# Loads at the heads of two attention stages: the first two units' loads are issued in front, ScalarE issues some of them, and group 0's keys come strip by strip

## The chip, the cores and the metric

One core of one Trainium2 chip runs the whole program. The metric is the device time of one execution in microseconds (us). The core has the engines PE (TensorE), DVE (VectorE), ACT (ScalarE), POOL (GpSimd) and SP (SyncE), and 16 DMA engines that all of them share. SP does nothing but issue DMAs; POOL and ACT can issue them too. Every engine runs its own instructions strictly in order, and a wait on a semaphore holds everything that is behind it on that engine.

## The reference

Two transformer layers over 4096 tokens of 256 features, 16 heads of 16. Layer 0 is a strided and local attention (each query sees every 8th key of the whole sequence and the keys of its own block of 128) beside an fp8 product; layer 1 is two dense causal attentions beside a mixture of experts. Cut to what the change touches:

```python
# layer 0, sparse: strided keys and the query's own block, one softmax over both
k_str = k[:, :, :Lg].reshape(B, Hn, ns, GBL, d)[:, :, :, -1, :]
w = softmax(einsum('bhnqd,bhnkd->bhnqk', fq, concat(k_str, k_local)) * scale + mask)
o = einsum('bhnqk,bhnkd->bhnqd', w, concat(v_str, v_local))
# layer 1, dense, twice (rotary q and k; normalised q and k)
scores = einsum('bhqd,bhkd->bhqk', Q, K) / sqrt(16);  causal mask;  softmax;  @ V
```

## The kernel before

The program has five stages that follow each other: embedding and the first projection, the sparse attention (`attend((0,), "sparse", ...)`), the middle projections, the two dense attentions (`attend((1, 2), "dense", ...)`), and the experts. At the end of each stage all five engines wait for all of its work and its stores (`stage_end`), so a stage's loads can't be issued before the stage ahead of it has stored its last bytes.

`attend` works on **units**: 4 heads (a group) of one strip of 512 queries. The sparse stage has 32 units (4 groups of 8 strips), the dense one 64. What a unit needs:

- its queries, in 6 DMAs of 64 KB (three terms for the odd and the even heads), into one of `held` buffers; in the sparse stage also its own keys (6 DMAs) and own values (1), which is 13 DMAs a unit;
- the keys and values of its group: strided keys and values in the sparse stage (`load_strided`, 7 DMAs a group, all four groups resident), the group's 4096 keys and values in the dense stage (two buffers; group 0's first strip of keys by 6 DMAs on SP, the other seven strips and the values by POOL, and group 1 by POOL as soon as unit 0 is weighed);
- rows of ones under the keys (`load_ones`, 2 rows for the odd and the even heads of each key tile) and mask halves (`load_halves`).

Each unit goes through two passes. First PE makes the unit's scores in **tiles** (L772 and L779 sparse, L783 dense), and DVE takes the maximum of each (L909, L913, L916). DVE negates the maxima, PE turns them (L788), DVE copies them to `neg_rows` (L937), and SP carries them by two small DMAs into two more rows of the unit's queries: this is the unit's **hand** (L713). Only then can PE make the scores again with the maximum already subtracted (L822, L832 sparse, L813 dense), ACT takes the exponential (L873) and PE multiplies by the values (L853). The list `order`, which all engines follow, lets the tiles run ahead of the second pass by `lead(n)` chunks. At the start of the sparse stage that is the 20 tiles of unit 0 and 8 of unit 1, at the start of the dense stage the 16 tiles of unit 0 and 24 of unit 1. In `order` a unit's first tile stands behind an entry `queries` for the next unit, at which SP issues that unit's loads; the hand of unit n stands at the sixth tile of unit n + 1.

## Time and profile before

| | |
|---|---|
| median of 3 runs | 5220.52 us (5220.5 to 5229.52) |
| the profiled execution | 5214.47 us, of which the span of the profile is 5212.6 us |
| busy share of the span | PE 91%, DVE 78%, ACT 54%, POOL 5% |
| sparse stage | from about 216 us to 840 us |
| dense stage | from about 1219 us to 4460 us |

The times in the profile count from the start of the span. "SPq" is SP's instruction queue issuing DMAs, and the granted clock (PEclk) is a share of 2.4 GHz, so 0.50 is 1.2 GHz and 1.00 is 2.4 GHz. A DMA's landing is the time when all of its bytes are counted in its semaphore.

### The profile page before, as it was taken

The numbers are of one execution on the slowest core, as the hardware profiler recorded it, in microseconds if no ns is written. First come the engines' busy times: TensorE is split into PE (matmuls) and PEld (weight loads), VectorE is DVE, ScalarE is ACT, GpSimd is POOL, SyncE is SP. The second block draws the span as 40 slices with busy tenths as digits, with TensorE's granted clock in tenths as the row PEclk, the third lists the DMA queues.
The fourth block names the chain that finished last, engine by engine and source line by source line (L and its number), as shares of the span: only waits on it lengthen the run. The fifth ranks groups of instructions, "written<-read, shape, count | busy, mean of one in ns | idle before, by whom it ended". The sixth has DMA issues, their size and how long they took to land.

```text
span 5212.6 us, 82823 instructions
## 1 busy us (share of the span) xinstructions
PE 4765.6 (91%) x31872; PEld 2545.8 (49%) x31872; DVE 4064.0 (78%) x9211; ACT 2835.7 (54%) x3309; POOL 270.1 (5%) x329
## 2 busy tenths in 40 slices
PE   5599997774999999999999999999999999899999
PEld 4455555662443334433334443334433333688888
DVE  7677775774888998889998889998889976455555
ACT  3255553221456766566766666766666776322322
POOL 2100001332000000000000000000000000200000
PEclk8699998776789999999999999999999999899999
DMA  5532322555300030300201300201300000210010
GB/s 162 171 79 66 70 69 83 187 175 145 58 13 13 7 55 23 54 9 9 46 12 23 54 9 9 46 12 23 54 9 9 5 9 11 70 41 21 21 41 9
DMA packets 256956, 258.37 MB, mean 50 GB/s; under 512 B 77224, under 2 KB 197032, under 8 KB 255016
## 3 DMA queue, kind: packets, MB, share of 16 engines
q1 hardware_dynamic: 250032, 211.50, 14.4%
q0 software_dynamic: 6528, 41.55, 5.0%
q8 instruction: 252, 4.13, 0.3%
q14 instruction: 144, 1.18, 0.1%
HBM read 145.43 MB, written 105.97 MB: 48 GB/s over the span
## 4 chain that ended last, share of the span: by engine, by line
PE 70%; DVE 18%; issue 5%; ACT 1%; DMA 1%; SPq 1%; POOL 0%; DVEq 0%; ACTq 0%; POOLq 0%
PE psum L853 23%; PE psum L783 19%; PE psum L76 13%; DVE maxes_dense L916 11%; PE psum L813 4%; PE psum L745 3%; PE psum L772 2%; PE psum L793 1%; PE psum L822 1%; PE psum L1596 1%; DVE masked_scores_dense L909 1%; PE psum L779 1%; PE psum L1197 1%; DMA queries_dense<-parts_scratch 1%; PE psum L1576 0%
## 5 line engine op out<-in xcount | busy, mean ns | idle before, releaser
L873 ACT ACTIVATE probs_dense<-psum 128x1024 f32<-128x1024 f32 (+3 forms) x2304 | 2068.2, 950 | 985.2 <-PE psum L813 741.8
L916 DVE TENSOR_REDUCE maxes_dense<-psum 128x1 f32<-128x512 f32 x3584 | 2226.7, 683 | 217.1 <-PE psum L783 216.2
L783 PE MATMUL psum<-keys,queries_dense 48*128 48x512 f32 (+3 forms) x4608 | 1551.1, 475 | 140.4 <-DMA queries_dense<-parts_scratch 56.2
L783 PEld LDWEIGHTS psum<-keys,queries_dense 48*128 48x128 f32 x4608 | 664.9, 190 | 1489.7 <-DVE maxes_dense L916 1137.8
L853 PE MATMUL psum<-probs_dense,values 128*32 128x512 f32 (+3 forms) x9216 | 1171.2, 586 | 0.0
L813 PE MATMUL psum<-queries_dense,keys 50*128 50x512 f32 (+3 forms) x4608 | 804.6, 405 | 12.2 <-ACT probs_dense L873 11.9
L909 DVE CUSTOM_DVE_ANT_0 masked_scores_dense<-psum,causal_add 128x128 f32<-128x128 f32 (+3 forms) x1024 | 452.4, 488 | 178.2 <-PE psum L783 159.2
L813 PEld LDWEIGHTS psum<-queries_dense,keys 50*128 50x128 f32 x4608 | 446.6, 192 | 107.3 <-ACT probs_dense L873 61.5
L909 DVE CUSTOM_DVE_ANT_0 masked_scores_sparse<-psum,after_add 128x512 f32<-128x512 f32 x512 | 326.1, 687 | 94.5 <-PE psum L772 93.5
L1703 ACT ACTIVATE activated<-psum 128x512 f32<-128x512 f32 x208 | 124.6, 599 | 417.6 <-PE psum L76 407.8
L853 PEld LDWEIGHTS psum<-probs_dense,values 128*32 128x32 f32 x9216 | 189.5, 109 | 270.9 <-issue 205.9
L873 ACT ACTIVATE probs_sparse<-psum 128x1024 f32<-128x1024 f32 x224 | 217.2, 1022 | 129.1 <-PE psum L745 51.8
L772 PE MATMUL psum<-str_keys,queries_sparse 48*128 48x512 f32 x512 | 176.2, 502 | 51.7 <-DMA str_values<-v_scratch 23.2
L1838 DVE CAST hid_high<-activated 128x512 fp32r<-128x512 f32 x208 | 92.2, 443 | 143.9 <-ACT activated L1703 140.9
L1840 DVE TENSOR_TENSOR hid_low<-activated,hid_high 128x512 fp32r<-128x512 f32 x208 | 150.4, 723 | 7.2
L772 PEld LDWEIGHTS psum<-str_keys,queries_sparse 48*128 48x128 f32 x512 | 70.7, 191 | 167.9 <-DVE maxes_sparse L909 88.2
L745 PE MATMUL psum<-tri_key,eye_bf 64*128 64x128 bf16 x2048 | 147.4, 223 | 0.0
L853 PE MATMUL psum<-probs_sparse,str_values 128*32 128x512 f32 x1024 | 142.4, 629 | 0.0
L873 ACT ACTIVATE probs_sparse<-psum,after_bias 128x1024 f32<-128x1024 f32 x96 | 101.6, 1112 | 66.1 <-PE psum L822 66.1
L822 PE MATMUL psum<-queries_sparse,str_keys 50*128 50x512 f32 x512 | 123.5, 450 | 1.5 <-ACT probs_sparse L873 1.3
L645 POOL DMA_DIRECT2D keys<-parts_scratch x48 | 24.1, 508 | 1931.5 <-PE psum L853 1917.7
L913 DVE TENSOR_REDUCE maxes_sparse<-psum 128x4 f32<-128x512 f32 x128 | 83.1, 688 | 44.5 <-PE psum L779 43.7
(295 smaller groups left out, 5350.6 us busy)
## 6 DMA issues: line engine op xcount, KB each, us to landing
v_scratch<-ve_s SPq DMA_DIRECT2D x96, 256.0 KB, 2.7
parts_scratch<-part_high SPq DMA_DIRECT2D x24, 1024.0 KB, 4.2
parts_scratch<-part_low SPq DMA_DIRECT2D x24, 1024.0 KB, 6.8
queries_dense<-parts_scratch SPq DMA_DIRECT2D x384, 64.0 KB
keys<-parts_scratch POOLq DMA_DIRECT2D x42, 512.0 KB, 18.0
values<-v_scratch POOLq DMA_DIRECT2D x8, 2048.0 KB, 34.9
queries_sparse<-parts_scratch SPq DMA_DIRECT2D x192, 64.0 KB
own_keys<-parts_scratch SPq DMA_DIRECT2D x192, 64.0 KB
```

Source lines behind the costliest of these rows:

```text
L76: m = pe.matmul(out_ap, left(l, c), right(r, c), start=(n == 0), stop=(n == len(pairs) - 1))
L745: m = pe.matmul(bank, eye2[own, part, :], addend, start=start and part == 0, stop=stop and part == 1)
L772: m = pe.matmul(bank, q[rows(h, TROWS), h // 2, b * P:(b + 1) * P], str_keys[n // STRIPS][rows(h, TROWS), h // 2, :], start=True, stop=True)
L783: m = pe.matmul(bank[:, 0:width], q[rows(h, TROWS), h // 2, b * P:(b + 1) * P], k[rows(h, TROWS), h // 2, kc * STRIP:kc * STRIP + width], ...
L813: m = pe.matmul(full[:, first_col:STRIP], k[own, h // 2, c * P:(c + 1) * P], q[own, h // 2, first_col:STRIP], start=True, stop=not diagonal)
L822: m = pe.matmul(full, str_keys[n // STRIPS][own, h // 2, c * P:(c + 1) * P], q[own, h // 2, :], start=True, stop=not partly)
L853: m = pe.matmul(psum[own_rows, 4, cols], vt, probs[(2 * m_at + h // 2) % 6][:, h % 2, cols], start=(c == 0), stop=(c == sizes[n] - 1 and b ...
L873: act.activation(probs[i % 6][:, :, first_col:STRIP], psum[:, at2:at2 + 2, first_col:STRIP], ACT.Exp, scale=SCALE, **extra).then_inc(exp_d ...
L909: m = dve.tensor_tensor_reduce(out=masked_scores[e % 2][:, 0:width], in0=bank[:, 0:width], in1=mask, scale=1.0, scalar=-3e38, op0=ALU.add, ...
L916: m = dve.tensor_reduce(mx[:, h * BLOCKS + b, kc:kc + 1], bank, AX.X, ALU.max)
L1703: act.activation(gs[k % 2][:], h_bank(u), func).then_inc(activated, 1)
L1840: dve.tensor_tensor(low[:, f, :], g[:], high[:, f, :].bitcast(F32), ALU.subtract).then_inc(hid_split, 1)
```

## The change

Five edits, all at the heads of the two attention stages:

1. SP issues the loads of unit 0 and unit 1 first in both stages, and from then on the entry `queries` for unit n + 1 issues the loads of unit n + 2. The sparse stage holds 6 units' tiles instead of 4 (the dense one held 8 already).
2. In the sparse stage ACT issues group 0's strided keys and values and all rows of ones (now 20 DMAs of ones, for 6 own key tiles); SP keeps the strided loads of groups 1 to 3.
3. In the dense stage group 0's keys come with the queries: each of the units 0 to 7 brings the strip of keys with its own number, by 6 more DMAs on SP. POOL's load of strips 1 to 7 is gone, and POOL issues group 0's values only when unit 1's loads have landed.
4. In the dense stage the masks and the ones are issued behind unit 1's loads, and PE waits for them at unit 0's second pass, no longer ahead of the first tile.
5. ACT issues the four weight loads ahead of the dense stage that SP issued before.

```diff
-        held = 4 if sparse else 8
+        held = 6 if sparse else 8
...
+                    if not sparse and n < STRIPS:
+                        load_keys(sp, 0, slice(j * STRIP, (j + 1) * STRIP), queries_in[n % 8])
...
+                load_queries(0)
+                load_queries(1)
                 if sparse:
-                    load_queries(0)
-                    load_strided(0)
-                    for tile in with_ones:
-                        load_ones(tile, ones_in)
                     for g in range(1, GROUPS):
-                        load_strided(g)
+                        load_strided(sp, g)
                 else:
                     for tile, name in halves:
                         load_halves(tile, name, masks_in)
                     for tile in with_ones:
-                        load_ones(tile, masks_in)
-                    load_keys(sp, 0, slice(0, STRIP), first_keys_in)
-                    load_queries(0)
+                        load_ones(sp, tile, masks_in)
                 for kind, n, what in order:
-                    if kind == "queries" and n < len(units):
-                        load_queries(n)
+                    if kind == "queries" and n + 1 < len(units):
+                        load_queries(n + 1)
...
-                else:
-                    pe.wait_ge(masks_in, 16 * mask_loads)
...
+                        if not sparse and n == 0:
+                            pe.wait_ge(masks_in, 16 * mask_loads)
...
             def attend_act():
                 if sparse:
+                    load_strided(act, 0)
+                    for tile in with_ones:
+                        load_ones(act, tile, ones_in)
                     act.wait_ge(bias_set, 1)
...
                 if not sparse:
-                    load_keys(pool, 0, slice(STRIP, TOKENS), keys_in[0])
+                    pool.wait_ge(queries_in[1], count_loaded(1))
                     load_values(pool, 0)
                     load(1)
...
-        sp.dma_start(tile, src).then_inc(final_weights, 16)
+        act.dma_start(tile, src).then_inc(final_weights, 16)
```

On SP at the head of the sparse stage, before: a unit's loads end with `own_values`, a group's strided loads with `str_values`. The stretch begins at the last own keys of unit 0.

```order
L679 DMA own_keys_0<-parts_scratch0_0 16x2x512
L681 DMA own_values_0<-v_scratch0 128x4x128
L658 DMA str_keys_0<-strided_scratch0 16x2x512
L658 DMA str_keys_0<-strided_scratch1 16x2x512
...
L660 DMA str_values_0<-v_scratch0 128x4x128
L637 DMA str_keys_0<-ones_scratch 2x2x512 x2
...
L637 DMA own_keys_3<-ones_scratch 2x2x512 x2
L658 DMA str_keys_1<-strided_scratch0 16x2x512
...
L660 DMA str_values_3<-v_scratch0 128x4x128
L672 DMA queries_sparse_1<-parts_scratch0_0 16x2x512 x2
```

The same place on SP now, with the way down to the hand of unit 0 (L721; L713 before).

```order
L691 DMA own_keys_0<-parts_scratch0_0 16x2x512
L693 DMA own_values_0<-v_scratch0 128x4x128
L682 DMA queries_sparse_1<-parts_scratch0_0 16x2x512 x2
...
L693 DMA own_values_1<-v_scratch0 128x4x128
L668 DMA str_keys_1<-strided_scratch0 16x2x512
...
L670 DMA str_values_3<-v_scratch0 128x4x128
L682 DMA queries_sparse_2<-parts_scratch0_0 16x2x512 x2
...
L682 DMA queries_sparse_3<-parts_scratch0_0 16x2x512 x2
...
L693 DMA own_values_3<-v_scratch0 128x4x128
L721 DMA queries_sparse_0<-neg_rows_sparse_0 2x8x128 x2
```

Unit 1's loads stand directly behind unit 0's, the strided loads of group 0 and the ones have left the queue, and four units' loads (before: three) stand ahead of the first hand.

On SP at the head of the dense stage, before, from the four weights of L1469 to the hand of unit 0.

```order
L1469 DMA lower<-in_c_lower 128x16
L146 DMA eye2_bf<-in_c_ident_bf 64x2x128 x2
L146 DMA tri_key2<-in_c_tri_key 64x2x128 x2
L637 DMA keys_0<-ones_scratch 2x8192 x2
L637 DMA keys_1<-ones_scratch 2x8192 x2
L645 DMA keys_0<-parts_scratch1_0 16x2x512
...
L672 DMA queries_dense_0<-parts_scratch1_0 16x2x512 x2
...
L672 DMA queries_dense_2<-parts_scratch1_1 16x2x512
L713 DMA queries_dense_0<-neg_rows_dense_0 2x8x128 x2
```

The same place on SP now; between the queries of each unit and the next stand six DMAs of keys (L655).

```order
L682 DMA queries_dense_0<-parts_scratch1_0 16x2x512 x2
...
L655 DMA keys_0<-parts_scratch1_0 16x2x512
L682 DMA queries_dense_1<-parts_scratch1_0 16x2x512 x2
...
L146 DMA eye2_bf<-in_c_ident_bf 64x2x128 x2
L146 DMA tri_key2<-in_c_tri_key 64x2x128 x2
L647 DMA keys_0<-ones_scratch 2x8192 x2
L647 DMA keys_1<-ones_scratch 2x8192 x2
L682 DMA queries_dense_2<-parts_scratch1_0 16x2x512 x2
...
L682 DMA queries_dense_3<-parts_scratch1_0 16x2x512 x2
...
L721 DMA queries_dense_0<-neg_rows_dense_0 2x8x128 x2
```

Ahead of the first tile's data SP had 18 other DMAs (4 weights, 4 masks, 4 ones and the 6 of the first key strip, which the tile needs) and now has none but the 12 that it needs; ahead of the first hand stand 48 loads of units and the 8 of masks and ones, before 4 + 8 + 6 + 18.

On POOL at the head of the dense stage, before and then now (the wait is in the diff).

```order
L645 DMA keys_0<-parts_scratch1_0 16x2x3584
L645 DMA keys_0<-parts_scratch1_1 16x2x3584
L645 DMA keys_0<-parts_scratch1_0 16x2x3584 x2
L645 DMA keys_0<-parts_scratch1_1 16x2x3584
L645 DMA keys_0<-parts_scratch1_0 16x2x3584
L650 DMA values_0<-v_scratch1 128x32x128
L645 DMA keys_1<-parts_scratch1_0 16x2x4096
```

```order
L660 DMA values_0<-v_scratch1 128x32x128
L655 DMA keys_1<-parts_scratch1_0 16x2x4096
```

The six large loads of group 0's keys are gone from POOL; group 1's follow as they did.

## Rows read from the trace of the kernel before

**Rows 1.** The page's part 4: the chain that ended last, by engine.

```profile
PE 70%; DVE 18%; issue 5%; ACT 1%; DMA 1%; SPq 1%; POOL 0%; DVEq 0%; ACTq 0%; POOLq 0%
```

**Rows 2.** The chain in order of time at the sparse head: start us, us, what.

```profile
224.65 3.05 DMA str_values<-v_scratch
...
227.84 0.81 PE psum L772 x2
...
242.54 11.71 issue
254.26 0.81 PE psum L772 x2
...
258.81 0.20 DVE neg_rows_sparse L937
...
259.72 1.94 DMA queries_sparse<-neg_rows_sparse
```

**Rows 3.** Timeline of SP's queue at the sparse head: start us, us, what, count.

```profile
215.79 2.66 SPq L672 DMA_DIRECT2D queries_sparse<-parts_scratch  x6
...
225.12 5.17 SPq L637 DMA_DIRECT2D str_keys<-ones_scratch  x8
...
235.34 2.73 SPq L658 DMA_DIRECT2D str_keys<-strided_scratch  x6
...
245.41 2.84 SPq L672 DMA_DIRECT2D queries_sparse<-parts_scratch  x6
...
251.55 2.83 SPq L672 DMA_DIRECT2D queries_sparse<-parts_scratch  x6
...
259.03 1.31 SPq L713 DMA_DIRECT2D queries_sparse<-neg_rows_sparse  x2
```

**Rows 4.** The chain in order of time at the dense head: start us, us, what.

```profile
1230.25 3.89 SPq L672
...
1237.25 28.80 DMA queries_dense<-parts_scratch
...
1266.28 0.49 PE psum L783 x2
...
1288.36 0.46 PE psum L813 x2
...
1293.98 1.86 PE psum L853 x8
```

**Rows 5.** Timeline of SP's queue at the dense head.

```profile
1219.45 0.37 SPq L1469 DMA_DIRECT2D wo<-in_L_ffn_wo  x1
...
1221.36 1.73 SPq L146 DMA_DIRECT2D eye_bf<-in_c_ident_bf  x2
...
1226.16 2.65 SPq L645 DMA_DIRECT2D keys<-parts_scratch  x6
1228.85 29.49 SPq L672 DMA_DIRECT2D queries_dense<-parts_scratch  x18
1278.63 1.41 SPq L713 DMA_DIRECT2D queries_dense<-neg_rows_dense  x2
```

**Rows 6.** Timeline of POOL at the dense head.

```profile
1223.20 1.72 POOL L650 DMA_DIRECT2D values<-v_scratch  x1
1302.00 2.98 POOL L645 DMA_DIRECT2D keys<-parts_scratch  x6 [77.08 <-PE psum L853]
```

**Rows 7.** Stretches: from:to and length, busy us by engine, PEclk, DMA share, GB/s.

```profile
1240.00:1245.00 5.00, 0.00 (x0) 0.00 (x0) 0.00 (x0) 0.00 (x0) 0.00 (x0) 0.50 1.00 117
...
1250.00:1252.00 2.00, 0.00 (x0) 0.00 (x0) 0.00 (x0) 0.00 (x0) 0.00 (x0) 0.50 1.03 375
...
1262.00:1264.00 2.00, 0.00 (x0) 0.00 (x0) 0.00 (x0) 0.00 (x0) 0.00 (x0) 0.50 0.08 27
```

**Rows 8.** Stretches, as above: a stretch of the sparse head, and one behind the dense head.

```profile
245.00:250.00 5.00, 0.00 (x0) 0.00 (x0) 0.00 (x0) 0.00 (x0) 0.00 (x0) 0.50 0.70 175
...
1300.00:1700.00 400.00, 389.15 (x2248) 164.73 (x2245) 352.29 (x718) 219.96 (x247) 16.70 (x23) 0.86 0.15 27
```

More of the change, by code:

```diff
@@ L518, in attend, with count_loaded, handed @@
         sparse = jobs == (0,)
-        held = 4 if sparse else 8
-        loads = 16 * (13 if sparse else 6)
-        per_unit = loads + 32
-        earlier = 0 if sparse else 4 * (16 * 13 + 32)
+        held = 6 if sparse else 8
+        per_unit = 16 * 15 if sparse else 16 * 8
+        earlier = 0 if sparse else 4 * 16 * 15
+        def count_loaded(n):
+            if sparse:
+                return per_unit * (n // 8) + 16 * 13
+            return earlier + per_unit * (n // 8) + 16 * 12
+        def handed(n):
+            return count_loaded(n) + 32
         groups = [(a, g) for a in jobs for g in range(GROUPS)]
@@ L598, in attend @@
                 keys_in, values_in = ([sem(f"{k}_in{i}") for i in range(2)] for k in ("keys", "values"))
-                first_keys_in, masks_in = sem("first_keys_in"), sem("masks_in")
+                masks_in = sem("masks_in")
             side_filled, side_freed = sem(f"side_filled_{stage}"), sem(f"side_freed_{stage}")
@@ L632, in attend, with load_ones @@
                 with_ones = keys
-            def load_ones(tile, loaded):
+            def load_ones(queue, tile, loaded):
                 for odd in range(2):
                     first_row = odd * HALF + TROWS
-                    sp.dma_start(tile[first_row:first_row + MROWS, :, :].bitcast(F32), ones_d[:, :, 0:tile.shape[2]]).then_inc(loaded, 16)
+                    queue.dma_start(tile[first_row:first_row + MROWS, :, :].bitcast(F32), ones_d[:, :, 0:tile.shape[2]]).then_inc(loaded, 16)
             def load_keys(queue, group, tokens, loaded):
@@ L650, in load_values, with load_strided @@
                 queue.dma_start(values[group % 2][:], v_d[a][g].rearrange("(b p) n -> p b n", p=P)).then_inc(values_in[group % 2], 16)
-            def load_strided(g):
+            def load_strided(queue, g):
                 for odd in range(2):
@@ L657, in load_strided @@
                         first_row = odd * HALF + i * HEAD_DIM
-                        sp.dma_start(str_keys[g][first_row:first_row + HEAD_DIM, :, :].bitcast(F32),
+                        queue.dma_start(str_keys[g][first_row:first_row + HEAD_DIM, :, :].bitcast(F32),
                                      src.rearrange("(h o e) t -> o e h t", o=2, e=HEAD_DIM)[odd]).then_inc(str_in[g], 16)
-                sp.dma_start(str_values[g][:], v_d[0][g].rearrange("(c p e) n -> p c e n", p=P, e=STRIDE)
+                queue.dma_start(str_values[g][:], v_d[0][g].rearrange("(c p e) n -> p c e n", p=P, e=STRIDE)
                              [:, :, STRIDE - 1, :]).then_inc(str_in[g], 16)
@@ L723, in wait_keys @@
                 group = n // STRIPS
-                if group == 0:
-                    pe.wait_ge(first_keys_in, 96)
-                    if n >= 1:
-                        pe.wait_ge(keys_in[0], 96)
-                else:
-                    pe.wait_ge(keys_in[group % 2], 96 * (group // 2 + 1))
+                if group >= 1:
+                    pe.wait_ge(keys_in[group % 2], 96 * ((group + 1) // 2))
             def attend_pe():
@@ L749, in attend_pe @@
                     pe.wait_ge(sparse_masks_in, SPARSE_MASKS)
-                else:
-                    pe.wait_ge(masks_in, 16 * mask_loads)
                 for kind, n, what in order:
@@ L765, in attend_pe @@
                         if what == tiles_of(n)[0]:
-                            pe.wait_ge(queries_in[n % 8], earlier + per_unit * (n // 8) + loads)
+                            pe.wait_ge(queries_in[n % 8], count_loaded(n))
                             if sparse:
@@ L935, in attend_dve @@
                         if n >= 2:
-                            dve.wait_ge(queries_in[(n - 2) % 8], earlier + per_unit * ((n - 2) // 8 + 1))
+                            dve.wait_ge(queries_in[(n - 2) % 8], handed(n - 2))
                         dve.tensor_copy(neg_rows[n % 2][:], psum[0:MROWS * GROUP * BLOCKS, 5 + e % 3, 0:P]).then_inc(side_freed, 1)
```

2 lines of the change are left out of this document (1 added, 1 removed).

## Prediction

> **What bounds the kernel now.** The page's chain first: 70% of the span goes over PE and 18% over DVE [rows 1]. So the long stretches of the five stages are bound by matmuls and maxima, which the change leaves alone: not one is added or taken away. What it can reach is the part of the chain that goes over DMAs and idle issue, and the chain in order of time shows that part in two places, the heads of the two attention stages.
>
> At the sparse head the chain runs over a landing at 224.65 + 3.05 = 227.70 us, then PE starts on the tiles of unit 0 at 227.84, is done with them at 242.54, and stands for 11.71 us until unit 1's loads have landed [rows 2]. SP's queue shows why these are late: unit 1's loads are issued from 245.41 on, behind the ones (from 225.12) and three groups' strided loads (from 235.34) [rows 3]. The second pass starts only when unit 0's hand has landed, at 259.72 + 1.94 = 261.66 [rows 2].
>
> At the dense head SP starts to issue at 1219.45 [rows 5] and PE at 1266.28, released by a load of queries that ends a wait of 28.80 us for the DMA alone [rows 4]. Here it is not SP that is slow at first: a single issue of L672 took 3.89 us [rows 4], and 18 of them 29.49 us [rows 5], where six issues took 2.66 us in the sparse stage [rows 3]. All 16 DMA engines were busy (share 1.00) while they moved only 117 GB/s [rows 7]; that is POOL's load of seven strips of keys, which was issued ahead of the queries and crowds them out. From 1288.36 on unit 0's second pass runs, and from 1293.98 on its values are used [rows 4].
>
> Both heads are behind a barrier of all engines, so a microsecond won at a head moves everything behind it, as long as no other wait takes its place. Each sum below therefore asks when the **second pass of unit 0** can start, since by then PE has done the same 28 (sparse) or 40 (dense) tiles in either kernel.
>
> **Sparse head.** SP's order is now unit 0, unit 1, three strided groups, unit 2, unit 3, hand of unit 0. A unit's 13 issues take 251.55 - 245.41 = 6.14 us, the three strided groups 245.41 - 235.34 = 10.07 us [rows 3]. Unit 0's loads have been issued at 215.79 + 6.14 = 221.9 and land some 3 us after their last issue (3.05 us is the row's value for such a landing [rows 2]), at about 224.7. Unit 1's are issued by 228.1 and land by 231. PE starts some 3 us sooner than at 227.84, needs 14.7 us for unit 0's tiles (242.54 - 227.84 [rows 2]), reaches 239.5, and finds unit 1 there: the stall of 11.71 us is gone. The turned maxima were ready 258.81 + 0.20 - 254.26 = 4.8 us after unit 1's first tile [rows 2], so now at about 244.3. But a new wait takes a share of it: SP is free for the hand only at 215.79 + 4 x 6.14 + 10.07 = 250.4. Before it issued the hand at 259.03 [rows 3], at once. The gain is 259.0 - 250.4 = 8.6 us, not the 15 that the data alone would give. As the hand now stands right behind 26 loads in the same queue, I take 8. The bounds: 14.7 if nothing stood ahead of the hand (259.0 - 244.3), and below, the case of the rivals in which ACT's issues slow SP's.
>
> What ACT now issues has cover. No row shows an issue on ACT. If it costs what SP's do (0.44 us for a strided one, 5.17 / 8 = 0.65 us for one of ones [rows 3]), its 7 strided DMAs are out at 219 and its 20 of ones at 232; at three times that the strided loads are out at 225 and the ones at 264, and only the ones would then be later than the hand. Its first exponential comes behind the hand.
>
> The DMA engines had a share of 0.70 at 175 GB/s while SP issued without a pause [rows 8], so issue time, not bandwidth, set the pace, and ACT's 7 large DMAs can overlap for some 3 us. The Trainium skill ("DMA: Bandwidth & Descriptors", section "Issuing engines are not separate DMA queues") says that DMAs from different engines run on the same 16 DMA engines and that issuing from several saves only the sequencer's time, which it calls usually small. By the rule taken alone this edit would win nothing; by the row the saved time is what counts, since the queue of issues is 34.6 us long. Both agree that only issue time can be saved, and the sum holds nothing else.
>
> **Dense head.** Twelve issues are needed for unit 0. Six take 1228.85 - 1226.16 = 2.69 us where nothing crowds them [rows 5], so twelve 5.4. They start at 1219.45, end at 1224.8, and land 3 us after their last issue, at 1227.5; I give ACT's four weights beside them half a microsecond. PE starts at 1228.0 in place of 1266.28: **38.3 us** sooner. Unit 1's loads are out at 1230.2 and land at 1233, while PE needs 8 us for unit 0's tiles.
>
> Then the hand. Behind unit 1 SP issues masks and ones in 1226.16 - 1221.36 = 4.8 us [rows 5], then unit 2 and unit 3 (5.4 each), and is free at 1245.8. Before, the hand was issued 1278.63 - 1266.28 = 12.4 us after the first tile [rows 4, 5], which would be 1240.4: again it waits in SP's queue. It lands 2.6 us after its issue (261.66 - 259.03 [rows 2, 3]), at 1248.4. PE comes to the second pass 1288.36 - 1266.28 = 22.1 us after the first tile [rows 4], at 1250.1. So on paper the delay is hidden with 1.7 us to spare.
>
> Two things can eat that. First POOL's values: 2 MB at the 375 GB/s of [rows 7] are 5.6 us, and they start at about 1235, as units 2 and 3 are issued. Second the ones: in the dense stage each is 64 KB in only two rows. After POOL's traffic the DMA share was 0.08, little more than one of 16 engines, while the last loads of SP were still outstanding [rows 7]; these landed at 1237.25 + 28.80 = 1266.05 [rows 4]. My reading is that the four DMAs of ones hold one or two engines for long, an estimate of 6 to 10 us, and that what SP issued behind them waits there. Now they stand behind units 0 and 1, which is a gain, but ahead of the hand: 1235 + 10 = 1245, then what is left of the loads of units 2 and 3 and of the values, and the hand lands at 1251 to 1255. I take 3 us of loss against 1250.1, with 0 and 9 as bounds. Values: needed 1293.98 - 1266.28 = 27.7 us after the first tile [rows 4], at 1255.7 or later; issued at 1233 to 1235 (1.72 us [rows 6]), they may land from 1242 to 1254. Before, they also carried no wait. Dense gain: 38.3 - 3 = **35 us**.
>
> **Costed at nothing.** The 6 further DMAs for units 2 to 7 cost SP 2.7 us each in a queue that otherwise waits for hands; their cover is the length of a unit. From unit 4 on they fall into POOL's load of group 1, which starts with the end of unit 0 (before at 1302.00 [rows 6]) as it did; unit 2's hand would be the first to suffer. Loading two units ahead needs a free buffer: by the order of the program each buffer is released by a product that PE has already passed, so SP waits for nothing new. Four weights on ACT lie 60 us ahead of its first exponential. PE's later wait for the masks is met at 1240.
>
> **Sum.** 8 + 35 = 43 us. The profiled execution took 5214.47 us, so it would be 5171.5; the median of the runs is 5220.52, 6 us more, and the forecast is 5220.5 - 43 = **5177.5 us**, 0.8% faster. Within 0.2% (some 10 us) a measurement of this kernel can't tell from no change.
>
> **The rivals.**
>
> *The dense hand is crowded out.* If the issues of unit 3 are held as SP's were before (3.89 us each [rows 4] in place of 0.45), twelve cost 41 us more and the dense gain is gone: 5220.5 - 8 = 5212. Against it: POOL's keys are not there, and 2 MB of values last a fifth of that. A part is likelier: 10 us lost give 5187. Together 14%.
>
> *ACT and SP get in each other's way as they issue.* If the hardware behind both took one issue at a time, ACT's 7 and 20 (3.1 + 13 us) would push the sparse hand to 266, 7 us later than before: 5220.5 + 7 - 35 = 5192. Nothing in this trace shows ACT issuing, for or against. 8%.
>
> *The first tile's data land no sooner,* since the stage's bytes must come in anyway. Then only the sparse 8 us are left, 5212. Against it: at the sparse head the same kind of loads landed in 3 us. 3%.
>
> *Slower: PE's clock.* It was granted 0.50 over both heads, and 0.86 on average from 1300 to 1700 [rows 8], with PE busy for 389 of 400 us. In the new kernel PE comes to this stretch with a shorter rest behind it. If the clock were granted less there, PE's time would grow in proportion: 400 x 0.86 / x - 400 exceeds 43 us when x falls under 0.777, and at 0.70 it would be 91 us, 5269 in all. Against it: the stretch holds the same matmuls in the same order. 3%.
>
> **How the numbers follow.** The forecast (36 to 52 us won, 5168 to 5185) has 70%, more than that 2%. The range 5165 to 5193 takes in the forecast, the partly crowded hand and the shared issue. Faster by over 0.2%: 0.93; within: 0.04; slower: 0.03.
>
> **What the profile after would show.** Right: PE's first L772 near 225 us and no long gap before unit 1's tiles; the sparse hand issued near 250 with SP never idle before it; dense first tile 8 to 9 us after SP's first issue of the stage; no issue of SP over 1 us before POOL's values; PE waiting a few microseconds for the dense hand; a clock from there on as before. Wrong: issues of 2 us and more on SP for units 2 and 3, a wait of PE for values, or issues on SP beside ACT's that are longer than 0.5 us. I am surest of the 38 us and least sure of the hand behind the ones.

## Result and the profile after

| | before | the changed kernel |
|---|---|---|
| median of 14 runs each | 5230.78 us (5207.63 to 5257.79) | 5198.48 us (5184.92 to 5222.99) |
| profiled execution, its span | 5214.47, 5212.6 us | 5203.78, 5201.9 us |
| ratio, 95% interval | | 0.9941 [0.9922, 0.9959] |

The change makes the kernel about 31 us faster (1 - 0.9941 of 5230.78; 41 to 21 by the interval), where 43 were forecast. In a later comparison (12 and 23 runs) the ratio was 0.9958 [0.9939, 0.9978], 22 us.

**Sparse head.** Timeline of SP's queue in the changed kernel, then of ACT's, then the two rows of PE at which the first tile and the second pass of unit 0 become possible (the bracket is the idle time before and its releaser):

```profile
215.78 2.67 SPq L682 DMA_DIRECT2D queries_sparse<-parts_scratch  x6
218.49 3.23 SPq L691 DMA_DIRECT2D own_keys<-parts_scratch  x6
221.76 0.59 SPq L693 DMA_DIRECT2D own_values<-v_scratch  x1
222.39 3.72 SPq L682 DMA_DIRECT2D queries_sparse<-parts_scratch  x6
...
230.55 3.27 SPq L668 DMA_DIRECT2D str_keys<-strided_scratch  x6
...
242.19 2.83 SPq L682 DMA_DIRECT2D queries_sparse<-parts_scratch  x6
...
254.49 1.51 SPq L721 DMA_DIRECT2D queries_sparse<-neg_rows_sparse  x2
```

```profile
215.81 2.74 ACTq L668 DMA_DIRECT2D str_keys<-strided_scratch  x6
218.59 0.45 ACTq L670 DMA_DIRECT2D str_values<-v_scratch  x1
219.07 5.60 ACTq L647 DMA_DIRECT2D str_keys<-ones_scratch  x8
224.70 7.85 ACTq L647 DMA_DIRECT2D own_keys<-ones_scratch  x12
```

```profile
229.91 1.19 PE L774 MATMUL psum<-str_keys,queries_sparse 48*128 48x512 f32 x3 [25.24 <-DMA own_values<-v_scratch]
...
257.43 0.80 PE L774 MATMUL psum<-str_keys,queries_sparse 48*128 48x512 f32 x2 [7.65 <-DMA queries_sparse<-neg_rows_sparse]
```

The stall for unit 1's loads is gone, and PE waits 7.65 us for the hand. But the first tile comes 2.1 us later than before (229.91 against 227.84 [rows 2]), and six issues on SP take 3.72 us beside ACT's, in place of 2.66. The wait for the hand ends at 257.4, before at 261.7 [rows 2]: 4.3 us won. Windows of before and then of the changed kernel (length, busy by engine, PEclk, DMA share, GB/s) show why the data come no sooner:

```profile
220.00:225.00 5.00, 0.00 (x0) 0.00 (x0) 0.00 (x0) 0.00 (x0) 0.00 (x0) 0.50 0.76 177
```

```profile
220.00:225.00 5.00, 0.00 (x0) 0.00 (x0) 0.00 (x0) 0.00 (x0) 0.00 (x0) 0.50 1.14 161
225.00:230.00 5.00, 0.09 (x2) 0.12 (x2) 0.00 (x0) 0.00 (x0) 0.00 (x0) 0.50 1.13 175
```

Two queues issue, the DMA engines are busier (a share of 1.14 in place of 0.76), and they move no more bytes in a second than one queue fed them before (161 and 175 GB/s in place of 177).

**Dense head.** SP's queue, POOL and PE in the changed kernel, then the one link of its chain that matters:

```profile
1218.48 2.66 SPq L682 DMA_DIRECT2D queries_dense<-parts_scratch  x6
...
1232.28 1.34 SPq L647 DMA_DIRECT2D keys<-ones_scratch  x4
1233.66 4.24 SPq L682 DMA_DIRECT2D queries_dense<-parts_scratch  x6
...
1246.70 1.41 SPq L721 DMA_DIRECT2D queries_dense<-neg_rows_dense  x2
```

```profile
1231.95 1.86 POOL L660 DMA_DIRECT2D values<-v_scratch  x1 [26.58 <-DMA keys<-parts_scratch]
```

```profile
1227.48 0.76 PE L785 MATMUL psum<-keys,queries_dense 48*128 48x128 f32 x3 [18.32 <-DMA keys<-parts_scratch]
...
1260.30 0.48 PE L785 MATMUL psum<-keys,queries_dense 48*128 48x128 f32 x2 [11.54 <-DMA queries_dense<-neg_rows_dense]
1260.57 0.74 PE L817 MATMUL psum<-queries_dense,keys 50*128 50x512 f32 x2
```

```profile
1247.44 12.81 DMA queries_dense<-neg_rows_dense
```

The same second-pass row of before, in PE's timeline, was

```profile
1287.89 1.00 PE L813 MATMUL psum<-queries_dense,keys 50*128 50x512 f32 x2
```

The first tile comes 9.0 us after SP's first issue of the stage (46.8 before), the hand is issued 19.2 us after the tile, and then these two DMAs of 8 KB take 12.81 us to land (counted here and below from the start of the second one's issue, where the chain has it). The second pass starts 42.1 us after SP's first issue (1260.57 - 1218.48), before 68.4 (1287.89 - 1219.45 [rows 5]): 26.3 us won. Both heads together: 4.3 + 26.3 = 30.6 us, which agrees with the runs (21 to 41 us).

**What the dense hand waits for.** The trace also keeps the time of each increment of each semaphore, and these show it. The loads in 16 rows and the values raise their semaphore 16 times for each DMA. The DMAs of two rows, the ones and the hand, raise it 3 times, once at the issue and twice later. In the changed kernel the last increment of the ones comes at 1247.43, just as the hand's second DMA is issued, so the hand doesn't wait for the ones themselves. But of the 16 increments of the values 14 have come by 1248.16 and the last two come at 1256.27 and 1256.53. The last of unit 2's loads comes at 1257.33, of unit 3's at 1259.89 and of the hand at 1260.25. Two parts of sixteen are 8 us behind, and the hand lands with them. In e9, the changed kernel once more, it is the same (14 by 1259.49, then 1266.89 and 1268.62), and in e12 below, where the ones have another shape, all 16 come between 1255.65 and 1258.04. The values' DMA as a whole shows it too: from its issue to its landing it takes 24.8 us in e9 and 15.4 in e12.

**Where the rest of the time went.** The two profiled executions differ by only 10.7 us, so 19.9 us of the 30.6 were lost outside the heads: 3.3 ahead of the dense head and 16.6 behind it. One stretch behind it, in before and then in the changed kernel:

```profile
3055.00:3230.00 175.00, 170.83 (x1142) 70.06 (x1144) 157.28 (x305) 119.98 (x133) 0.00 (x0) 0.98 0.03 7
```

```profile
3055.00:3230.00 175.00, 171.25 (x1063) 69.48 (x1063) 150.22 (x292) 114.56 (x126) 0.00 (x0) 0.91 0.05 10
```

PE is as busy in both, but at 0.91 of full speed in place of 0.98 it does 1063 matmuls in place of 1142. In the profiled execution of e9 14.8 us were lost much earlier, between the hands of units 5 and 7 of the sparse stage. The times of all runs follow their mean granted clock: of the changed kernel's 14 runs the fastest (5184.92 us) had 0.932 and the slowest (5222.99 us) 0.924. So the spread of 38 to 50 us in the times of either kernel goes with the clock, and the experiments are read by distances within the heads, where the clock is 0.50; a single time says little.

### The profile page after: what moved, and what is told of

Read it like the earlier page. It is cut to its first block, busy times and chain, and to the rows that moved or that the text cites. A ratio compares the mean times of both kernels' runs of the same rounds, so it can differ in the third digit from the quotient of the medians.

```text
span 5201.9 us, 82855 instructions
## 1 busy us (share of the span) xinstructions
PE 4783.6 (92%) x31872; PEld 2548.6 (49%) x31872; DVE 4063.9 (78%) x9211; ACT 2836.0 (55%) x3309; POOL 268.0 (5%) x323
## 3 DMA queue, kind: packets, MB, share of 16 engines
q1 hardware_dynamic: 250304, 212.87, 14.5%
## 4 chain that ended last, share of the span: by engine, by line
PE 71%; DVE 18%; issue 4%; ACT 1%; SPq 1%; DMA 1%; POOL 0%; DVEq 0%; ACTq 0%; POOLq 0%
PE psum L857 23%; PE psum L785 19%; PE psum L76 13%; DVE maxes_dense L923 11%; PE psum L817 4%; PE psum L749 3%; PE psum L774 2%; PE psum L795 1%; PE psum L826 1%; PE psum L1603 1%; DVE masked_scores_dense L916 1%; PE psum L781 1%; PE psum L1204 1%; PE psum L1583 0%; PE psum L836 0%
## 5 line engine op out<-in xcount | busy, mean ns | idle before, releaser
L817 PE MATMUL psum<-queries_dense,keys 50*128 50x512 f32 (+3 forms) x4608 | 807.1, 406 | 11.8 <-ACT probs_dense L880 11.5
L826 PE MATMUL psum<-queries_sparse,str_keys 50*128 50x512 f32 x512 | 122.8, 450 | 1.5 <-ACT probs_sparse L880 1.3
L920 DVE TENSOR_REDUCE maxes_sparse<-psum 128x4 f32<-128x512 f32 x128 | 83.2, 688 | 45.1 <-PE psum L781 44.3
L655 POOL DMA_DIRECT2D keys<-parts_scratch x42 | 20.8, 503 | 1891.6 <-PE psum L857 1891.4
```

The costliest lines, as they stand in the source:

```text
L817: m = pe.matmul(full[:, first_col:STRIP], k[own, h // 2, c * P:(c + 1) * P], q[own, h // 2, first_col:STRIP], start=True, stop=not diagonal)
L826: m = pe.matmul(full, str_keys[n // STRIPS][own, h // 2, c * P:(c + 1) * P], q[own, h // 2, :], start=True, stop=not partly)
```

## The experiments

All kernels are the changed one but for the edit shown, and each was run once, but for e8 and e9. Where PE didn't wait for the hand (before, e1, e6, e8), its landing is the last increment of its semaphore. Dense head, us; "from SP" is from SP's first issue of the stage, the others from PE's first tile:

| kernel | first tile from SP | hand issued | hand landed | second pass | second pass from SP |
|---|---|---|---|---|---|
| before | 46.8 | 12.4 | 15.0 | 21.6 | 68.4 |
| changed | 9.0 | 19.2 | 32.8 | 33.1 | 42.1 |
| changed, again (e9) | 9.7 | 18.3 | 32.9 | 33.2 | 42.9 |
| e1 ones behind the hand | 9.2 | 18.0 | 21.6 | 32.0 | 41.2 |
| e2 values behind the hand | 9.6 | 17.1 | 22.5 | 22.8 | 32.4 |
| e3 unit 3 behind the hand | 9.3 | 12.8 | 30.1 | 30.4 | 39.7 |
| e5 ones by strip | 8.9 | 23.1 | 25.7 | 26.0 | 34.9 |
| e6 values at once | 15.1 | 12.4 | 18.7 | 21.6 | 36.7 |
| e10 half the ones | 9.5 | 17.3 | 25.9 | 26.2 | 35.8 |
| e12 ones spread | 9.8 | 21.2 | 24.7 | 25.0 | 34.9 |
| e8 five moves together | 10.1 | 14.1 | 16.6 | 22.9 | 33.0 |

The edits of e4, e7 and e11 leave the dense head as it is, and there its second pass comes 42.6, 41.2 and 43.1 us after SP's first issue, so a distance of this head varies by 2 us.

Sparse head, us from SP's first issue of the stage:

| kernel | first tile | hand issued | second pass (L822, now L826) |
|---|---|---|---|
| before | 12.1 | 43.2 | 46.5 |
| changed (e9) | 14.1 (14.4) | 38.7 (40.1) | 42.2 (43.5) |
| e3 unit 3 behind the hand | 14.2 | 33.5 | 38.9 |
| e4 ones from 18 us on | 12.8 | 37.7 | 45.1 |
| e7 16 of 20 ones behind the hand | 14.0 | 35.5 | 41.8 |
| e11 ACT issues nothing | 12.5 | 50.7 | 54.1 |
| e8 five moves together | 14.1 | 33.4 | 36.8 |

In the six dense experiments that leave this head as it is, its second pass comes 41.9 to 44.0 us after SP's first issue. So the change wins 2.5 to 4.6 us here, and a difference of 2 us between two kernels says nothing.

**e1: the ones of the dense keys behind the first hand**

```diff
-                    for tile in with_ones:
-                        load_ones(sp, tile, masks_in)
...
+                        if not sparse and n == 0:
+                            for tile in with_ones:
+                                load_ones(sp, tile, masks_in)
```

> Dense head only: the four DMAs of ones are issued behind the hand of unit 0, not ahead of the loads of units 2 and 3. In the changed kernel the hand was issued at 1246.70 and landed at 1260.25, 32.8 us after PE's first tile, where 22.1 us would have kept PE busy. Theory A (the ones hold the two DMA engines that the hand also needs): the hand is issued some 1.3 us sooner and lands within 5 us of its issue, by about 23 us after the first tile; PE then waits for the ones, not for the hand, some 10 us more, so the second pass starts about where it did. Theory B (the loads of units 2 and 3 and the values crowd the hand): the hand still lands 10 us or more after its issue. Theory C (issue time on SP): it lands 1.3 us sooner, no more.

5204.75 us. The hand lands 21.6 us after the tile, 2.9 us after its last issue, with the values and the loads of units 2 and 3 where they were; so these alone don't make it late. But the second pass needs the ones too, and they are slow behind it. PE and the chain:

```profile
1272.68 0.47 PE L786 MATMUL psum<-keys,queries_dense 48*128 48x128 f32 x2 [10.53 <-DMA keys<-ones_scratch]
```

```profile
1261.56 11.03 DMA keys<-ones_scratch
```

Four DMAs of 64 KB take 11 us from their last issue, while the last of the keys, as large each and in 16 rows, landed in 3.98 us in the same run. By the increments the four land one after the other, at 1265.56, 1268.09, 1270.53 and 1272.60.

**e2: POOL issues the values behind the first hand**

```diff
-                    pool.wait_ge(queries_in[1], count_loaded(1))
+                    pool.wait_ge(queries_in[0], handed(0))
```

> Dense head only: POOL issues group 0's values (2 MB) when the hand of unit 0 has landed. Theory A (ones): the hand still lands 10 us or more after its issue, at most 3 us sooner than the 32.8 us after the first tile. Theory B, for its part on values: it lands within 5 us, some 8 to 10 us sooner. In either case the products of unit 0 wait for values, by about 8 us after the hand's landing, so the time as a whole is not better than the changed kernel's.

5169.15 us. The ones stand where they stood, and the hand lands after 4.64 us, 22.5 after the tile; then the values are late. The chain:

```profile
1248.40 4.64 DMA queries_dense<-neg_rows_dense
...
1253.68 10.12 DMA values<-v_scratch
```

So the ones alone are done by the time of the hand (their last increment is at 1247.02). It takes the values as well to make it late.

**e3: unit 3's loads behind the first hand, in both stages**

```diff
-                    if kind == "queries" and n + 1 < len(units):
+                    if kind == "queries" and n != 2 and n + 1 < len(units):
...
+                        if n == 0:
+                            load_queries(3)
```

> Both heads: the loads of unit 3 are issued behind the hand of unit 0, not ahead of it. Sparse: the hand goes out when its rows are ready, about 249, not at 254.49, and the second pass starts about 5 us sooner, at 252. Dense: the hand is issued near 1241 (relative to a stage start at 1218.48; 12 us after the first tile). Theory A (ones): it lands when the ones are through, 27 to 31 us after the first tile, against 32.8, since fewer loads stand between. Theory B (loads and values crowd it) the same or better, 23 to 27. Theory C (SP's issue time alone was what made it late): 15 to 18 us after the first tile, and PE doesn't wait for it at all.

5210.46 us. In the dense stage the hand is issued 6.4 us sooner after the tile and lands 2.7 us sooner (16.54 us under way): it isn't SP's queue that decides there. In the sparse stage the same move wins 3.3 us at the second pass (38.9 against 42.2, and 3.0 against the lowest of the unchanged heads).

**e5: each unit's strip of dense keys brings its own ones**

```diff
+                        for odd in range(2):
+                            first_row = odd * HALF + TROWS
+                            sp.dma_start(keys[0][first_row:first_row + MROWS, :, j * STRIP:(j + 1) * STRIP].bitcast(F32),
+                                         ones_d[:, :, 0:STRIP]).then_inc(queries_in[n % 8], 16)
...
-                    for tile in with_ones:
-                        load_ones(sp, tile, masks_in)
...
+                        if not sparse and n == 0:
+                            sp.wait_ge(masks_in, 64)
+                            load_ones(sp, keys[1], masks_in)
```

> Dense head: the rows of ones of group 0's key tile come strip by strip, two DMAs of 8 KB with each unit's keys, and those of the other key tile (128 KB) only behind the hand of unit 0. So two rows' worth of 32 KB less each, four times, stands on the two DMA engines ahead of the hand; the values stay as they were. Earlier runs gave for the hand's landing, counted from PE's first tile: 32.8 us in the changed kernel, 30.1 with the hand issued 6 us sooner, 22.5 with the values issued behind it. Theory F (ones and values add up on two engines, either one's removal frees the hand): the hand lands 22 to 25 us after the first tile, and PE waits 3 us at most. Theory B alone (the values' packets slow everything by themselves): 28 us or later. The second pass of unit 0 would start 8 to 10 us sooner than the changed kernel's 33.3 us after the first tile under F, 3 us or less under B.

5184.48 us. With the values where they were and only 8 KB of ones in a DMA (two DMAs a unit), the hand is issued 23.1 us after the tile and lands at once:

```profile
1255.20 1.87 DMA queries_dense<-neg_rows_dense
```

**e6: POOL issues the values without a wait**

```diff
-                    pool.wait_ge(queries_in[1], count_loaded(1))
```

> Dense head: POOL issues group 0's values at once, without the wait for unit 1's loads. Under theory F the 2 MB pass while units 0 and 1 are loaded: the first tile comes later than the 9.0 us after SP's first issue that the changed kernel has, by up to 8 us, and the hand then finds the engines free but for the ones: it lands within 6 us of its issue. Sum: second pass of unit 0 at 36 to 40 us after SP's first issue of the stage, against 42.3 in the changed kernel. If the values crowd out the first loads as group 0's keys did in the kernel before (SP's issues of 3 us and more), it is 45 or later.

5211.4 us. The first tile pays 6 us (15.1), and the second pass is yet 5.4 us sooner from SP's first issue (36.7 against 42.1): the values' last increment comes at 1243.99, while the ones are being issued (1242.70 to 1244.03), and PE doesn't wait for the hand at all.

**e10: half the ones.** keys_1's two DMAs behind the first hand, keys_0's two in place.

> Of the dense stage's four large DMAs of ones only keys_0's two stand ahead of unit 2's loads; keys_1's two go behind the first hand. Theory A (the large two-row DMAs hold the engines on which they run, and their time adds to the values' ahead of the hand): half the ones, about half of their 11 us gone, so the hand of unit 0 lands 26 to 29 us after the first tile (changed kernel 32.8) and PE waits 5 to 8 us in place of 11.5. Rival (the values and the loads of units 2 and 3 alone make the hand late): it lands 31 to 33 us after the first tile as before. A second rival (any two-row load ahead is enough, whatever its size): the same 31 to 33.

5181.15 us. The hand lands 25.9 us after the tile, 6.9 us sooner; PE waits 4.70 us.

**e12: the same ones, in the same place, in another shape.** 8 DMAs of one row in 16 pieces (1x16x512) in place of 4 of two rows (2x8192):

```diff
+                        for odd in range(2):
+                            for r in range(MROWS):
+                                row = odd * HALF + TROWS + r
+                                sp.dma_start(tile[row:row + 1, :, :].bitcast(F32).rearrange("s h (b c) -> s (h b) c", c=512),
+                                             ones_d.rearrange("s g t -> (s g t)").rearrange("(o c e) -> o c e", o=1, e=1024)[:, :, 0:512]).then_inc(masks_in, 16)
```

> The same 256 KB of ones for the dense keys, at the same place in SP's queue, but as 8 DMAs of one row in 16 pieces (1x16x512) in place of 4 of two rows (2x8192). Computes the same. Theory A (the bytes of a two-row DMA run on very few DMA engines, and the hand, two rows too, waits there): in 16 pieces the ones are spread and cost nothing; SP issues four more DMAs (about 1.5 us), so the hand is issued 20 to 21 us after the first tile and lands 2 to 5 us behind, 22 to 26 us after the tile, PE waits 0.5 to 4 us (changed kernel 32.8 and 11.5). Rival (the bytes ahead of the hand and the values crowd it, whatever their shape): it lands 32 to 34 us after the first tile, as in the changed kernel.

5179.95 us. SP's queue, PE and the chain:

```profile
1241.92 5.55 SPq L714 DMA_DIRECT2D keys<-ones_scratch  x8
...
1259.23 1.41 SPq L725 DMA_DIRECT2D queries_dense<-neg_rows_dense  x2
```

```profile
1262.73 0.47 PE L789 MATMUL psum<-keys,queries_dense 48*128 48x128 f32 x2 [3.47 <-DMA queries_dense<-neg_rows_dense]
```

```profile
1259.98 2.70 DMA queries_dense<-neg_rows_dense
```

The same 256 KB in the same place of the queue, with the values beside them, and the hand lands 2.70 us after its last issue in place of 12.81. The issues cost more (0.69 us each in place of 0.34), and PE waits 3.47 us. The shape was the cause, not the number of bytes. (The new DMAs also read their source in pieces of 2 KB with gaps; this wasn't tried apart from the spread.)

**e4: ACT's ones only when unit 1's loads have landed (sparse)**

```diff
                     load_strided(act, 0)
+                    act.wait_ge(queries_in[1], count_loaded(1))
```

> Sparse head only: ACT issues group 0's strided loads at once, but its 20 DMAs of ones only when unit 1's loads have landed. In the changed kernel SP's issues of unit 1 took 8.16 us beside ACT's ones, against 6.14 before, and own_values landed only at 229.8. Theory D (issues from two engines slow each other): SP's issues for unit 1 take 6.2 us again, unit 0's tiles start 2 to 4 us sooner than 229.91, and the hand is issued 3 to 4 us sooner than 254.49 if ACT's ones don't then slow the strided groups instead; if they do, 0 to 1 us. Theory E (the DMA engines are the limit, not the issuing): SP's issues stay at 0.57 us each.

5224.68 us. SP's timeline in this run, ahead of ACT's ones and then while ACT issues them (234.43 to 247.90):

```profile
222.23 2.83 SPq L682 DMA_DIRECT2D queries_sparse<-parts_scratch  x6
...
239.02 3.72 SPq L682 DMA_DIRECT2D queries_sparse<-parts_scratch  x6
```

The longer issues move with ACT's ones. The hand is issued 1.0 us sooner but takes 6.00 us to land (2.04 in the changed kernel), so the head as a whole loses 2.9. Here too two parts of sixteen lag: of a weight load that SP issued right behind the hand 14 increments have come by 257.72 and the last two come at 260.75 and 261.75. The first tile comes 1.3 us sooner than in the changed kernel, so ACT's ones are the larger part of the 2.1 us that it lost.

**e7: ACT issues 4 of the ones, the other 16 behind the first hand (sparse)**

```diff
+                    for tile in (str_keys[0], keys[0]):
+                        load_ones(act, tile, ones_in)
+                    act.wait_ge(queries_in[0], handed(0))
...
+                    for tile in str_keys[1:] + keys[1:]:
+                        load_ones(act, tile, ones_in)
```

> Sparse head: ACT issues the strided loads of group 0 and only the 4 DMAs of ones that unit 0 needs; the other 16 when unit 0's hand has landed. Theory D (issues of small two-row DMAs on ACT make SP's issues longer, 0.57 to 0.60 us in place of 0.43 to 0.47): nearly all of SP's issues go back to 0.43 to 0.47 us, the hand is issued 34.5 to 35.5 us after SP's first issue of the stage, against 38.7, and lands within 3 us; the second pass starts 3 to 4 us sooner than in the changed kernel. The first tile stays where it is, 13 to 14 us after SP's first issue (12.05 in the kernel before), if the DMA engines limit the landing of unit 0's 20 loads. Theory E (issuing isn't what is slowed): the hand's issue stays within 1 us of 38.7.

5229.54 us. SP is back at 0.43 to 0.47 us an issue and issues the hand 3.2 us sooner, but it takes 4.79 us to land, and the second pass gains 0.4, which is nothing clear. No two parts lag clearly here (the 16 increments of the same weight load come from 255.09 to 257.42); the DMA engines had a share of 1.08 at 203 GB/s (250 to 255 us), and the hand lands at 257.24, just after unit 3's loads at 256.86. Then ACT's first exponential stands behind its 16 issues, and unit 0's outputs are ready 14.5 us later than in the changed kernel (74.8 against 60.3 us after SP's first issue).

**e11: ACT issues nothing at the sparse head; SP does all**

```diff
                 load_queries(0)
+                if sparse:
+                    load_strided(sp, 0)
                 load_queries(1)
+                if sparse:
+                    for tile in with_ones:
+                        load_ones(sp, tile, ones_in)
```

> At the sparse head ACT issues nothing; SP issues unit 0, group 0's strided loads, unit 1, the 20 ones and from there on as the changed kernel. Theory D (issue time counts, and SP's issues lengthen only beside ACT's): SP's issues fall back to 0.45 us, but 27 more stand in its queue; 4 units at 6.14, 4 strided groups at 3.3 and 20 ones at 0.65 us are 51 us, so the hand is issued 50 to 52 us after SP's first issue (changed kernel 38.7), lands 3 us behind, and the second pass starts at about 269.5 us, 12 us later than in the changed kernel and 8 later than before the change. Rival (the bytes ahead of the hand set its landing, whoever issues them): the second pass starts at 257 to 259 us.

5216.9 us. The hand is issued 50.7 us after SP's start, and the second pass starts at 270.82. Issue time in front of the hand does count: ACT's 27 issues would take SP 16.1 us (3.34 + 12.72 in this run) and moving them to ACT brings the hand 12.0 sooner.

**e8: five moves together, beside the changed kernel (e9), 12 runs each.** Ones by strip as in e5; unit 3's loads behind the hand as in e3; the strided groups 1 to 3 one each behind the hands of units 0 to 2; the values as soon as unit 0's loads have landed, not unit 1's:

```diff
-                    pool.wait_ge(queries_in[1], count_loaded(1))
+                    pool.wait_ge(queries_in[0], count_loaded(0))
...
+                        if sparse and n + 1 < GROUPS:
+                            load_strided(sp, n + 1)
```

> Computes the same as the changed kernel. Five moves beside it: in the dense stage each unit's strip of keys brings its own 8 KB of ones (4 rows in two DMAs), the other key tile's large ones go behind the first hand; unit 3's loads go behind the first hand in both stages; the strided groups 1 to 3 of the sparse stage are loaded one each behind the hands of units 0 to 2; POOL issues the values once unit 0's loads have landed, not unit 1's. Theory A (the large two-row ones, and what is queued in the DMA engines ahead of the hand, set its landing): the dense second pass starts 31 to 33 us after SP's first issue of the stage (changed kernel 42.3), the sparse hand is issued about 34 us after SP's first issue (changed kernel 38.7) and the second pass of unit 0 comes about 5 us sooner than in the changed kernel. Together 10 to 15 us under the changed kernel, a ratio to before of 0.991 to 0.992. Rival (the hand's place decides nothing, each head is bound by the stage's bytes): second passes at the same distances as in the changed kernel, and the same time as it within 0.1%.

> The changed kernel again, on the same chip as the kernel above, so that the two can be compared: 0.992 to 0.996 of before, as in its first runs, with the dense second pass 42 us and the sparse one 41 to 42 us after SP's first issue of the stage.

e8: 5203.4 us, ratio to before 0.9928 [0.9902, 0.9955]; e9: 5214.96 us, 0.9958 [0.9939, 0.9978]. The heads of e8 win 35.4 + 9.7 = 45.1 us over before, those of e9 25.5 + 3.0 = 28.5; both lie in their intervals. By the heads e8 is 16.6 us faster than the changed kernel, by the medians 11.6, but the intervals overlap, so the times alone don't tell them apart. Time multiplied by the run's granted clock does, as it takes out most of the spread: on average 4823.4 for e9 and 4815.1 for e8, 8.4 apart with a standard error of 2.3, where 16.6 us at a clock of 0.50 would be 8.3. At the dense head PE no longer waits for the hand; unit 1's ones hold it for 1.96 us, and DVE's maxima set the rest of the way:

```profile
1236.10 0.77 PE L791 MATMUL psum<-keys,queries_dense 48*128 48x128 f32 x3 [19.46 <-DMA keys<-ones_scratch]
...
1245.02 1.19 PE L791 MATMUL psum<-keys,queries_dense 48*128 48x512 f32 x3 [1.96 <-DMA keys<-ones_scratch]
...
1258.98 1.00 PE L825 MATMUL psum<-queries_dense,keys 50*128 50x512 f32 x2
```

## Why the prediction was too high

**Dense first tile, 38.3 us: right.** 8 to 9 us after SP's first issue were forecast and 9.0 came, so the tile is 37.8 us sooner (46.8 - 9.0). That POOL's load of seven strips was what had crowded the queries out is argued and not shown alone: in the kernel before, of the 96 increments of unit 0's queries 84 came by 1259.29 and the last 12, two of sixteen for each DMA, only from 1264.81 to 1266.04. So some 7 us of its 46.8 are the two lagging parts behind the ones, and the change took away both at once. ACT's four weights cost nothing visible.

**The dense hand, "3 us of loss, with 0 and 9 as bounds": the step that failed.** The mechanism was named, the ones ahead of the hand and then the values, but its size was not. The loss was 33.1 - 21.6 = 11.5 us, above my upper bound. I had the hand wait until 1245 for the ones and let what is left of units 2 and 3 and of the values follow until 1251 to 1255. The ones did end near there (1247.43), but what follows took until 1260.25. Behind the ones the values and the units' loads had piled up on the engines that carry them, by the increments two of sixteen, and I had priced that rest without this. So the two add up: ones without values ahead leave the hand at 22.5 (e2), values without ones at 21.6 (e1, hand issued at 18.0), both together at 32.8, half the ones at 25.9. And e12 shows that it is the shape: cut in 16 pieces, the same ones cost the hand nothing beyond their issue time. A row that the prediction had in hand, a share of 0.08 while the last loads were outstanding [rows 7], pointed there. I read it as one or two engines busy, and then did not ask on which engines the hand itself, also two rows, would run.

The Trainium skill ("DMA: Bandwidth & Descriptors", section "Why a DMA increments its semaphore by 16 and not by 1") says that a DMA from SP or ACT is cut over the largest number of engines, up to 16, that divides the slowest dimension of both sides, and always takes the lowest-numbered ones. By that rule ones of two rows and hands of two rows share the same two engines, and 1x16x512 spreads over 16. The runs agree (12.81 against 2.70 us for the hand, 3 increments for a DMA of two rows and 16 for the others, two of sixteen parts of the values late); the trace doesn't name the engines.

How the two add up can be estimated from the bytes in these runs. If a DMA of two rows is halved and the others are cut in 16, each of two engines has 128 KB of ones, 96 KB of units 2 and 3 and 8 KB of the hand in e2, 232 KB in the 18.3 us from the first issue of the ones (1234.78) to the hand's landing (1253.04). At that rate the changed kernel, with 128 KB of values more, needs 28.3 us, and 28.0 were measured; e10 (296 KB) needs 23.3 us against 21.7 measured, and e3 (312 KB) 24.6 against 25.6.

**Sparse, 8 us: mis-sized, 4.3 came.** The term was SP free for the hand at 250.4; it was free at 254.49. 2.5 of the 4.1 us were lost over units 0 and 1 (230.55 - 215.78 = 14.8 us in place of 12.3) and 1.6 over the strided groups. The 2.5 are the rival "ACT and SP get in each other's way", in part: SP's issue went from 0.43 to 0.59 us beside ACT's ones, while ACT's own came every 0.70 and 0.65 us. e4 and e7 show that this lengthening goes with ACT's ones (beside ACT's strided loads SP's issues in e4 keep 0.42 us). Most of the 1.6 us is something else: one group of six took 4.01 us from 237.67 on, after ACT's last issue (232.55) but while its ones were still landing (until 240.17); with most ones held back (e7) or all on SP (e11) it took 2.83. What slows SP there stays open. e11 shows that moving them off SP still pays, 11.9 us at the second pass. That the first tile would come 3 us sooner was wrong too: it came 2.1 us later, which costs nothing, as the hand decides.

For the sparse head I set the row against a rule of the Trainium skill ("DMA: Bandwidth & Descriptors", section "Issuing engines are not separate DMA queues"): the DMAs of all issuing engines run on the same 16 DMA engines, and issuing from several saves only the sequencer's time, usually a small one. The trace agrees with the first part, as the two queues together moved 161 to 175 GB/s where one had moved 177, and with the second, as issue time was saved; but here it is not small (12.0 us). What the sum missed is that an earlier issue isn't an earlier landing: e4 and e7 issue the hand sooner than the changed kernel and it then takes 6.00 and 4.79 us to land in place of 2.04, in e4 with two parts lagging, in e7 with a DMA share of 1.08.

**Costed at nothing.** Right for the six further DMAs a unit, the wait for the masks, the weights on ACT, and loading two ahead: between the heads no new wait appears. In the sparse stage the hands of units 1 to 4 come at the same distances from the second pass in both kernels, to 0.1 us; in the dense stage 23.8 of the 26.3 us are still won at the hand of unit 11. **The clock** has a part in the missing 2.5 us: from the hand of unit 6 to that of unit 7, with the same 501 matmuls in the stretch, it was granted 0.92 before (86.5 us) and 0.88 in the changed kernel and in e9 (88.3 and 88.2 us). As there is one profile of the kernel before, it isn't shown that the change brings this about. The larger losses of clock wander from run to run.

**The sum.** 12.4 us are missing from 43: 8.7 at the dense head (35 against 26.3) and 3.7 at the sparse one. The kernel before also took 5230.78 us in these runs, 10 more than the base of the forecast; on that base a ratio of 0.9941 is 5189.7 us, inside the range of 5165 to 5193, in place of the 5198.48 measured.

## What to carry to other kernels

A small DMA on the critical path needs more than a free queue: look at the shape of what is in flight ahead of it. Cut long transfers of one or two rows into 16 pieces, or issue them where nothing small follows, and add up what such an engine has to carry, with any large load beside them. Moving issues to a second engine was worth about three quarters of their time in the first queue here (12.0 of 16.1 us), and the first tile's bytes landed no sooner for it. Two versions that differ in a stage's head are best compared by distances from the stage's first issue, as those agreed within about 2 us where whole times spread over 40.

## What the runs showed of the hardware that was unexpected

- Four DMAs of 64 KB in two rows took 11.03 us to land from their last issue; the same bytes as eight of 1x16x512 left the hand behind them landing in 2.70 us, at twice the issue time each (0.69 against 0.34 us).
- SP's issue of a 64 KB DMA took 0.43 us alone and 0.59 us while ACT issued small two-row DMAs.
- A DMA of two rows raised its semaphore 3 times, one of 16 rows 16 times; behind the ones two of the 16 increments of a 2 MB load came 8 us after the other 14.
- 2 MB of values took 10.12 us when they were issued behind the hand (e2), 15.4 us beside SP's loads with the ones spread (e12) and 24.8 us with the ones in two rows (e9).
